# The start of a macaron block on one core: who quantises w2, when the sum of |w2| is taken, and two small steps moved ahead of it

## What is computed

```
def _bit_quant(w):
    scale = jnp.maximum(jnp.mean(jnp.abs(w)), EPS)
    w_ternary = jnp.clip(jnp.round(w / scale), -1.0, 1.0)
    return w + jax.lax.stop_gradient(w_ternary - w)
w1q = _bit_quant(w1)          # w1: 1024 x 256
w2q = _bit_quant(w2)          # w2: 256 x 1024
h = jnp.einsum('bsd,fd->bsf', x, w1q) + b1
h = jax.nn.gelu(h, approximate=False)
return jnp.einsum('bsf,df->bsd', h, w2q) + b2
...
x = x + 0.5 * _L0_ffn_ref(_layernorm(x, axis=-1), ...)
x = x + _L0_attn_ref(_layernorm(x, axis=-1), ...)
x = x + 0.5 * _L0_ffn_ref(_layernorm(x, axis=-1), ...)
```

## Time and the profile before

| what | value |
|---|---|
| median of 3 runs | 702.36 us (700.59 to 702.56) |
| the profiled execution | 701.41 us |
| its span, first to last instruction | 699.6 us |
| PE busy in the span | 629.8 us (90%) |
| DVE busy | 483.4 us (69%) |
| ACT busy | 341.1 us (49%) |
| POOL busy | 260.3 us (37%) |
| mean granted clock of TensorE | 0.968 |

### The profile page before, as it was taken

How to read it: one execution, slowest core, us unless ns; L and a number is a source line. 1 busy time by engine, 2 the same in 40 slices (tenths; PEclk the granted TensorE clock), 3 DMA queues, 4 the chain that set the end, 5 groups by cost and what they waited for, 6 DMA issues and landing times. The chain is left out here.

```text
span 699.6 us, 15227 instructions
## 1 busy us (share of the span) xinstructions
PE 629.8 (90%) x4932; PEld 514.8 (74%) x4932; DVE 483.4 (69%) x978; ACT 341.1 (49%) x623; POOL 260.3 (37%) x472
## 2 busy tenths in 40 slices
PE   1899999999769877569999999999999789999997
PEld 1698888888657666247777777777777568888886
DVE  5977777779869865646666666666666367777764
ACT  2344544453433334236566665666655544444443
POOL 3834434427778875412111111111111134433330
PEclk9999999999998899689999999999999999999999
DMA  8310000000897776923333333333331000000011
GB/s 270 125 56 1 0 0 0 0 0 5 226 312 219 213 201 185 252 61 110 115 98 92 92 91 109 114 97 92 91 111 30 2 1 30 30 30 30 30 46 45
DMA packets 71599, 63.18 MB, mean 90 GB/s; under 512 B 4790, under 2 KB 64790, under 8 KB 71574
## 3 DMA queue, kind: packets, MB, share of 16 engines
q1 hardware_dynamic: 70390, 62.72, 30.8%
q10 hardware_dynamic: 1184, 0.14, 0.2%
HBM read 33.03 MB, written 29.36 MB: 89 GB/s over the span
## 5 line engine op out<-in xcount | busy, mean ns | idle before, releaser
L866 ACT ACTIVATE probs<-bank 128x512 f32<-128x512 f32 x192 | 114.2, 597 | 89.0 <-PE bank L942 75.4
L827 DVE TENSOR_REDUCE mx<-bank 128x2 f32<-128x512 f32 (+1 forms) x192 | 127.9, 688 | 12.1 <-PE bank L920 8.4
L386 PE MATMUL bank<-w2q,g_hi 128*128 128x256 f32 x512 | 124.7, 285 | 3.0 <-DVE g_lo L286 2.6
L386 PE MATMUL bank<-w2q,g_lo 128*128 128x256 f32 x512 | 123.0, 281 | 0.0
L343 ACT ACTIVATE g<-bank,b1c 128x512 f32<-128x512 f32 x128 | 88.2, 689 | 70.0 <-PE bank L381 66.6
L386 PEld LDWEIGHTS bank<-w2q,g_hi 128*128 128x128 f32 x512 | 97.0, 189 | 4.6 <-DVE w2q L293 2.1
L386 PEld LDWEIGHTS bank<-w2q,g_lo 128*128 128x128 f32 x512 | 97.1, 190 | 0.7
L286 DVE TENSOR_TENSOR g_lo<-g,g_hi 128x512 fp32r<-128x512 f32 x128 | 86.2, 704 | 3.6
L381 PE MATMUL bank<-xt_hi,w1q 128*128 128x512 f32 x256 | 82.1, 402 | 1.7 <-PEq L677 1.7
L381 PE MATMUL bank<-xt_lo,w1q 128*128 128x512 f32 x256 | 81.5, 400 | 0.0
L240 POOL TENSOR_TENSOR res<-res,b2h 128x1024 f32 (+1 forms) x16 | 38.9, 2431 | 83.6 <-DVE xn L131 64.8
(11 more groups left out here) (102 smaller groups left out, 1226.4 us busy)
## 6 DMA issues: line engine op xcount, KB each, us to landing
qk_slots<-parts SPq DMA_DIRECT2D x32, 384.0 KB, 3.8
q<-qk_slots SPq DMA_DIRECT2D x32, 384.0 KB, 3.9
k<-qk_slots SPq DMA_DIRECT2D x32, 384.0 KB, 4.6
qk_slots<-parts SPq DMA_DIRECT2D x32, 256.0 KB, 3.4
res<-x SPq DMA_DIRECT2D x8, 512.0 KB, 3.5
qk_slots<-parts SPq DMA_DIRECT2D x32, 128.0 KB, 3.2
out<-res SPq DMA_DIRECT2D x8, 512.0 KB, 2.9
q<-mt SPq DMA_DIRECT2D x96, 4.0 KB
```

The costliest lines, as they stand in the source:

```text
L386: last = nc.tensor.matmul(y_bank[t % 2][:, 0:D], part[:, f, t * P:(t + 1) * P], w2q[:, f, :], start=f == 0 and part is g_hi, stop=f == FC ...
L827: nc.vector.tensor_reduce(o, i, AX.X, ALU.max).then_inc(s_done, 1)
L866: nc.scalar.activation(probs[g % 2][:, 512 * u:512 * u + 512], t_ring[(3 * g + u) % 2][:], ACT.Exp, scale=0.25)\
```

## The change

- `round_xt(act, 0)` stands ahead of the four sums of |w2| on ACT.
- On PE the mean of w2 is no longer taken ahead of the first GEMM but inside it, ahead of block f = 2.
- On DVE the reduction of the sums of w2 (L278) comes after the second half of w1, not between the halves. `threshold(1)` follows as before.
- The four `is_lt` of w2 go from POOL to DVE, each directly ahead of its second step. The pieces come at f = 0, 1, 2 and 3 of the first chunk, no longer at 1, 3, 5 and 7; pieces 0 and 1 come ahead of the first rounding of g.
- `ln_stats(1)` of the first chunk goes from the chunk's beginning to f = 4.
- POOL waits for the first half of w1q in place of the thresholds of w2, and goes on to `residual(0)` and then to the moments of chunk 1.

```
-                        pool.wait_ge(s_thr, 4)
-                        for k in range(4):
-                            pool.tensor_scalar(tern[1][:, k * 512:(k + 1) * 512], raw[1][:, k * 512:(k + 1) * 512],
-                                               thr[:, 1, 1:2], None, ALU.is_lt).then_inc(s_low, 1)
                         pool.wait_ge(b2_ready, 1)
+                        pool.wait_ge(s_quant, 1)
...
                             if half == 0:
                                 split_xt(dve, 0)
-
-                                dve.wait_ge(s_fold2, 4)
-                                nc.vector.tensor_reduce(wtot[:, 1:2], wsum2[:], AX.X, ALU.add).then_inc(s_tot, 1)
+                        dve.wait_ge(s_fold2, 4)
+                        nc.vector.tensor_reduce(wtot[:, 1:2], wsum2[:], AX.X, ALU.add).then_inc(s_tot, 1)
                         threshold(1)
...
                     def ternary_w2(k):
                         piece = slice(k * 512, (k + 1) * 512)
+                        if k == 0:
+                            dve.wait_ge(s_thr, 4)
+                        nc.vector.tensor_scalar(tern[1][:, piece], raw[1][:, piece], thr[:, 1, 1:2], None, ALU.is_lt).then_inc(s_low, 1)
                         dve.wait_ge(s_low, k + 1)
...
-                            ln_stats(following)
+                            if not first:
+                                ln_stats(following)
                         for f in range(FC):
+                            if first and f < 2:
+                                ternary_w2(f)
+                            if first and f == 4:
+                                ln_stats(following)
                             if f in BY_DVE:
...
                             if f > 0:
-                                if first and f % 2 == 1:
-                                    ternary_w2(f // 2)
+                                if first and f in (2, 3):
+                                    ternary_w2(f)
                                 low_part(gc, f - 1)
...
+                        round_xt(act, 0)
                         act.wait_ge(w2_in, 32)
                         for k in range(4):
                             nc.scalar.activation(g[:, k, :], raw[1][:, k * 512:(k + 1) * 512], ACT.Abs,
                                                  accum_out=wsum2[:, k:k + 1]).then_inc(s_fold2, 1)
-                        round_xt(act, 0)
...
+                    def mean_of(m):
+                        pe.wait_ge(s_tot, m + 1)
+                        nc.tensor.matmul(y_bank[m][:, 0:1], ones_mean[:], wtot[:, m:m + 1], start=True, stop=True)\
+                          .then_inc(s_mean, 1)
...
                         for f in range(FC):
+                            if f == 2 and first:
+                                mean_of(1)
...
-                        for m in range(2):
-                            pe.wait_ge(s_tot, m + 1)
-                            nc.tensor.matmul(y_bank[m][:, 0:1], ones_mean[:], wtot[:, m:m + 1], start=True, stop=True)\
-                              .then_inc(s_mean, 1)
-                            if m == 0:
-                                transpose_x(pe, 0)
+                        mean_of(0)
+                        transpose_x(pe, 0)
```

## The result

| kernel | median of 6 runs | lowest to highest |
|---|---|---|
| before | 701.97 us | 700.59 to 703.28 |
| changed | 705.19 us | 704.13 to 705.94 |

The ratio is 1.0045 (95% interval 1.003 to 1.006). Forecast were 702.0 us, a range to 704.0, and 0.75 for no change: the time lies above the range. The profiled execution of the changed kernel took 705.70 us with a span of 703.8 us.

What follows compares the result with a forecast made beforehand. It took PE's GEMM of chunk 1 (41.33 us) to wait for late POOL and DVE. Early start mostly lost to statistics and clock left 0.1 us: 701.3 from the profiled execution, 702.0 forecast nearer the median, range 699.8 to 704.0.

Steps and rivals of the forecast that it cites:

- Part 1: ACT's rounding ahead of the sums of w2: PE's first GEMM begins at 16.0, 1.5 us ahead of 17.52.
- Part 2: Bias early on POOL: its residual delays DVE's second half of w1; w2's reduction ends at 19.3, in time for PE's 19.6.
- Part 3: Mean of w2 inside PE's first GEMM: takes 0.45 us at no cost; DVE's first comparison of w2 at about 20.65.
- Part 4: Comparisons of w2 on DVE: its remaining list takes 12.4 us, to 33.0; added 1.8 us paid by meetings that go away.
- Part 5: POOL's moments of chunk 1: begin at 29.1, take 4.75 us, end at 33.9; ln_apply gains 0.6 us.
- Part 6: PE and its clock before chunk 1's GEMM: between a gain of 0.4 and a loss of 0.2, taken as 0.1 us gain.
- (b): Rival: clock stays low, second half of chunk 1's matmuls all at 1.2 GHz, mark at 44.2, 705.2 us; chance 0.24.
- variant in which the transposes don't count: Clock counts only from 36.8, rises at 39.9, 13 matmuls slow, 702.3 to 703.2 us; a third of its rival's chance.
- (a): Rival: the early start carries through, moments near 2.79 us, transposes at 2.4 GHz; 2.1 us gain, 700.3 by median; chance 0.17.
- (c): Rival: w2's reduction misses PE's f = 2, or comparisons take 0.75; nothing gained, 702.4 to 703.5 us; chance 0.12.

Runs made afterwards that it cites:

- own_wait: Changed kernel plus one DVE wait for its own g_lo signal behind block 3, before the next cast; 700.17 us, 0.9976 of before.
- pause_full: Changed kernel plus a DVE wait behind the statistics at f = 4 until all eight POOL operations of the moments are done; 702.74 us, 1.0007 of before.
- swap: Changed kernel with the first two POOL operations of the moments in the other order; 704.13 us, 1.0029 of before.
- psum_break: Changed kernel plus one unused DVE copy of 256 columns from PSUM behind the cast at f = 5; 703.69 us, 1.002 of before.
- pause_two: Changed kernel plus a DVE wait behind the statistics at f = 4 until POOL's first two moments operations are done; 700.88 us, 0.998 of before.
- stats_gap: Changed kernel with the statistics of chunk 1 moved on DVE between the reduction of w2 and the thresholds; 699.51 us, 0.9962 of before.

## Why the prediction was wrong

**Part 1 was right.** The first GEMM begins 5.29 us behind the reduction of w1; forecast 16.0 - 10.72 = 5.28.

**Part 2 was right.** POOL's residual (14.48 to 16.85) holds DVE's comparison of w1, 1.95 us in place of 0.75, and the mean comes to PE's f = 2 in time: DVE waits for PE there, not the reverse.

**Part 3 was near.** The mean takes 0.28 us of PE, not 0.45; DVE is at w2 at 20.26, not 20.65, most of it because PE came to the mean at 19.34, not 19.6.

**Part 4 was right, in part by luck.** The comparison of 512 columns takes 0.48 to 0.49 (taken: 0.42, bounds 0.42 and 0.75), and the list takes 12.6 us for 12.4; it ends at 32.89, forecast 33.0, because it also began 0.4 early.

**Part 5 failed, and with it the prediction.** "I take 4.75, the nearer" was a price from a stretch in which POOL got in between DVE's instructions, and its upper end was the same 4.75. Measured were 6.57, of which 3.99 for the first operation. This is what the price was read from, in the kernel before:

```profile
29.27 0.65 POOL L104 TENSOR_TENSOR both<-stats 128x8 f32<-128x8 f32 x1
29.88 0.38 POOL L105 TENSOR_TENSOR apart<-stats 128x4 f32<-128x4 f32 x1
30.34 0.58 POOL L107 TENSOR_TENSOR apart<-apart 128x4 f32<-128x4 f32 x1
31.01 0.51 POOL L109 TENSOR_SCALAR variance<-both 128x4 f32<-128x4 f32 x1
```

Each of these ends within 0.1 us of the end of one DVE instruction of the earlier trace rows: POOL waited for one at a time, and in the changed kernel for eight. Neither the casts nor the g_lo were new, and DVE's run from 29.78 to 34.60 has no idle time in it either. The difference lies in what came before: there POOL was at work and had just held DVE's g_lo (3.49 us for two), here DVE had run for 2.75 us since its last wait for its own result (ahead of 26.21) when POOL asked at 28.96. That this is why is inferred; no run changes it alone. That POOL had been idle for 12 us is not the reason: in own_wait it had been too. pause_full shows that DVE does it, swap that the operation doesn't matter, psum_break that a DVE operation which reads PSUM lets POOL in, own_wait that one short wait ends it. xn came 1.6 us later than forecast (1.8 counted from the reduction of w1). The step also named what would be late, "they now wait for the statistics", and stopped there: it did not ask what POOL would meet at that moment.

**Part 6 failed in size.** I had the clock rise at 37.2 to 38.5, at most 3.1 us behind the start of unbroken work; it rose at 42, 4.9 us behind the transposes at 37.00, and the second half took 5.36 us. Without the hold the clock can be up again before the transposes (own_wait: granted 0.55 in 32 to 34, 1.00 in 34 to 36), though in pause_two it was not. With the hold there is a hole of 2.4 to 3.1 us ahead of them, and in all three executions without filling (changed, swap, psum_break) part of the transposes or all of them, and part of the second half, ran at 1.2 GHz, at a cost of 1.4 to 2.3 us. Among the versions of the changed kernel a slow second half came only with the hold. Its price, 2.29 in the changed kernel's execution, is in part chance.

**The rivals.** (b) names the clock, with a mark at 44.2 and 705.2 us. That this is what came (43.98 and 705.19) is luck: by its mechanism xn should not have been late and all 32 matmuls slow, while xn was 1.27 us later than before and 15 of the 32 were slow. Its chance of 0.24 and the top of the range at 704.0 were too low, since it needed no more than larger holes, which Part 6 itself had found. Its variant in which the transposes don't count is not settled: it had the clock rise 3.1 us behind the start of the second half, and it rose 3.3 behind it in the changed kernel, 2.5 in psum_break and 1.3 in swap. (a) took the moments at 2.79 and a high clock. own_wait and stats_gap come to the same state, DVE's list decides and the clock is up at the transposes, with moments of 4.14 and 4.13, and gave 700.2 and 699.5. (c) did not happen. The rule on the shared port pair changed nothing in Part 2, as said; the mistake was to apply it to the large operation of POOL and not to the small ones of Part 5. As the Trainium skill states it ("SBUF — State Buffer", section "SBUF: two separate sides"), the pair is held for one whole instruction. The trace of the changed kernel goes further than that: POOL waited 3.99 us, through eight DVE instructions in a row.

## What to carry to other kernels

Moving small operations next to a dense run on the other engine can cost what is left of the whole run (3.99 us here, where one instruction takes 0.42 or 0.68): ask of each moved instruction not only when it may start but what its partner engine does then, and whether anything breaks that engine's run. A price measured beside "the same work" holds only if the two engines also meet in the same way: here two runs of DVE, equally dense, let POOL in after each instruction or not at all. And when a late engine leaves PE a hole, add the clock to the price, as a range: against own_wait 2.3 to 2.4 us of delay cost 3.7 (swap), 3.9 (psum_break) and 4.7 us (changed) at the mark.

## What the runs showed of the hardware

A POOL operation of 0.20 us was held for 3.99 us (three kernels, to the hundredth) while DVE ran g_lo (two inputs from SBUF) and casts from SBUF back to back, and it ended with the last of them. An operation of DVE that reads PSUM let it in, for as long as it lasted (psum_break, once). A stop of DVE of 0.12 us, for its own signal, let it in too, and after such a stop the following POOL operations got in at the ends of DVE's instructions (0.20 to 1.36 us each), though these were as dense as before. In the kernel before, POOL operations got in at each instruction's end (0.28 to 0.65 us for those that take about 0.20 alone) without any stop of DVE in those 4.8 us, behind a meeting in which POOL had held DVE. What state the stop or the meeting changes, and why the third operation in psum_break was held again right after the copy, is open; that the wait or its gap is what matters is shown only by pause_two and own_wait, and for the `is_lt` by inference from where the operations end.
